# A router and attention kernel with its list building spread over five rounds ahead of the experts instead of four

## What is computed

```python
xn = layernorm(x)
# attention over the 4 heads of the same token, D = 256 per head
q, k, v = (xn @ W + b for W, b in ((Wq, bq), (Wk, bk), (Wv, bv)))
scores = (q*cos . k*cos + q*sin . k*sin) / 16      # per token, head x head
s = softmax(scores) @ v ; s = s.swapaxes(1, 2).reshape(...) @ Wo + bo
# mixture of 8 experts, 2 per token
g = sinkhorn((xn @ router_w.T + router_b) / temp)  # 3 iterations over 8 rows of a sequence
vals, idx = top_k(g, 2) ; w = vals / (sum(vals) + 1e-8)
y = sum_k w[k] * ((relu(xn @ wg[idx]) * (xn @ wp[idx])) @ wo[idx])
out = x + s * silu(xn + y)
```

## Time and profile before

| what | value |
|---|---|
| median of 3 runs | 1592.52 us (1590.27 to 1592.82) |
| profiled execution, its own time | 1590.1 us |
| its span | 1588.3 us |
| TensorE matmul busy | 1530.9 us, 96% |
| VectorE, ScalarE, GpSimd busy | 972.8, 728.8, 793.0 us |
| list matmuls | 128 |

### The profile page before, as it was taken

The page is one execution under the profiler, slowest core; times in us unless marked ns, Lnnn a source line. Parts: engine busy times, 40 slices in busy tenths (PEclk is TensorE's granted clock), DMA queues, the critical chain, the costliest instruction groups (busy, mean ns, idle before and its releaser), DMA issues.

```text
span 1588.3 us, 32794 instructions
## 1 busy us (share of the span) xinstructions
PE 1530.9 (96%) x11408; PEld 1166.3 (73%) x11408; DVE 972.8 (61%) x1880; ACT 728.8 (46%) x1205; POOL 793.0 (50%) x945
## 2 busy tenths in 40 slices
PE   5999699989999999999999999999999999999997
PEld 2546566668888888888888888776666776666773
DVE  7567989953333333333333333577889788888777
ACT  4766334413333333333333333546456565555552
POOL 4637589813433444433444333253574564853456
PEclk9999899989999999999999999999999999999999
DMA  9989852265233231323211231255555666455464
GB/s 327 396 314 324 301 187 78 76 217 189 68 124 108 82 126 64 97 95 111 77 54 57 71 146 51 90 167 166 172 187 189 205 200 207 156 168 172 155 206 147
DMA packets 175351, 251.23 MB, mean 158 GB/s; under 512 B 15336, under 2 KB 122656, under 8 KB 175072
## 3 DMA queue, kind: packets, MB, share of 16 engines
q1 hardware_dynamic: 160576, 211.48, 39.1%
q0 software_dynamic: 12960, 35.41, 6.8%
q10 hardware_dynamic: 1664, 2.26, 0.4%
HBM read 149.58 MB, written 99.50 MB: 157 GB/s over the span
## 4 chain that ended last, share of the span: by engine, by line
PE 89%; DVE 6%; DMA 2%; ACT 1%; issue 1%; SPq 1%; ACTq 0%; DVEq 0%
PE ps L1145 23%; PE ps L1080 21%; PE ps L1091 13%; PE ps L1164 12%; PE ps L1027 6%; PE ps L1154 4%; PE ps L1048 2%; PE ps L1127 2%; PE ps L996 2%; PE ps L924 1%; DMA WR<-w_d 1%; PE ps L980 1%; PE ps L914 1%; DVE UN L1230 1%; SPq L502 1%
## 5 line engine op out<-in xcount | busy, mean ns | idle before, releaser
L1145 PE MATMUL ps<-WR,FR 128*128 x1620 | 407.9, 401 | 1.9 <-DMA WR<-w_d 1.8
L1145 PEld LDWEIGHTS ps<-WR,FR 128*128 128x128 f32 x1620 | 296.2, 189 | 60.2 <-issue 3.0
L649 POOL DMA_INDIRECT y_d<-AUX x135 | 133.3, 987 | 351.6 <-ACT AUX L868 351.6
L1656 DVE TENSOR_TENSOR AUX<-AUX,ps 128x512 f32<-128x512 f32 x135 | 92.9, 688 | 342.0 <-ACT AUX L856 342.0
L817 ACT ACTIVATE WM<-ps,bcs,trig 128x512 f32<-128x512 f32 x256 | 252.2, 1016 | 85.9 <-PE ps L1080 78.9
L1596 DVE TENSOR_SCALAR WM<-ps,vec,trig 128x512 f32<-128x512 f32 x256 | 243.6, 993 | 61.2 <-ACT WM L817 60.5
L1091 PE MATMUL ps<-WM,XTJ 128*128 128x512 f32 x512 | 237.1, 600 | 0.0
L856 ACT ACTIVATE AUX<-ps 128x512 f32<-128x512 f32 x135 | 80.9, 599 | 318.5 <-PE ps L1145 318.5
L1080 PE MATMUL ps<-XH,WH 128*128 128x512 f32 x512 | 204.8, 400 | 6.1 <-issue 3.8
L1164 PE MATMUL ps<-WR,ABR 128*128 x1080 | 209.4, 292 | 0.0
L1080 PE MATMUL ps<-XH,WL 128*128 128x512 f32 x512 | 199.7, 390 | 0.0
(11 more groups left out here) (238 smaller groups left out, 2199.1 us busy)
## 6 DMA issues: line engine op xcount, KB each, us to landing
US<-u_d SPq DMA_DIRECT2D x63, 512.0 KB, 5.4
u_d<-UN SPq DMA_DIRECT2D x120, 256.0 KB, 2.0
WR<-w_d SPq DMA_DIRECT2D x96, 256.0 KB, 6.0
AUX<-y_d SPq DMA_DIRECT2D x32, 512.0 KB, 5.6
WM<-in_L_attn_x_dram SPq DMA_DIRECT2D x16, 512.0 KB, 9.5
xn_d<-WM SPq DMA_DIRECT2D x32, 256.0 KB, 7.3
w_d<-USR SPq DMA_DIRECT2D x16, 512.0 KB, 4.9
AUX<-xn_d SPq DMA_DIRECT2D x16, 512.0 KB, 6.1
```

What stands on the lines that cost most here:

```text
L649: e.indirect_dma_start(y_d, bass.IndirectOffsetOnAxis(toks[:, m - 5:m - 4], 0), YS[:, (m - 5) % 2, :], None).then_inc(s_y[(m - 5) % 2], 16)
L1145: mm = e.matmul(b[:, :], x, WR[:, bass.ds(off[m] + (2048 * z + 1024 * a + 512 * k), 512)], start=(k == 0 and x is xh and z == 0), stop=(k ...
L1656: e.tensor_tensor(HS[:, m % 2, :], GR[:, :], mP[m % 2][:, :], ALU.mult).then_inc(s_h, 1)
```

## The change

QE goes from 4 to 5, and a new QF = 4 keeps the old meaning for the outputs that are made good later: only rounds 0 to 3 are hosted, and round 4 stands ahead of the experts but is finished like the later ones, from round 5 on. In round 4 the U chunks (with the mixes of round 3) come first and the QK chunks last. In rounds 0 to 4 ScalarE writes both halves of chunks 2, 6, 10 and 14, and VectorE leaves them out. The second choice is cut in seven steps, six behind chunks 0 to 5 of round 1 and the gate weights behind chunk 16; the rank matmuls move from behind chunk 1 to behind chunk 8 of round 1, the rank steps to chunks 11 and 13, the slot steps to chunks 0 and 3 of round 2. The list matmuls start at chunk 6 of round 2 and run to chunk 13 of round 4, at most half a matmul for each group of scores. The translation stands behind chunk 15 of round 4, the selectors behind chunks 1, 5, 9 and 13 of round 3, and the permutation behind chunk 20 of round 3, in a bank of its own. Expert 0 is loaded as soon as chunk 23 of round 4, now its eighth, is done.

```diff
-QE = 4
+QE = 5
+QF = QE - 1
+        def order(q):
+            return [*range(16, 24), *range(16)] if q == QE - 1 else list(range(24))
+        def at(q, c):
+            return 24 * q + order(q).index(c) + 1
+        def lone(q, c):
+            return q < QE and c in (2, 6, 10, 14)
...
-            if (q, c) >= (1, 20):
-                pace += 1.5 if c < 16 else 2.4 if c < 24 else 4.0
+            if k >= 34:
+                pace += 1.57 if c < 16 else 2.6 if c < 24 else 0.5
...
-            e.wait_ge(s_ch, 24 * QE)
+            e.wait_ge(s_ch, at(QE - 1, 23))
             load_expert(0)
...
+                            if lone(q, c):
+                                e.activation(rotated(2 * x + 1, i), b, ACT.Identity, bias=bcs[:, x, 1, i:i + 1],
+                                             scale=trig[:, 1, i:i + 1])
...
-            side[24 + 1] = sink_end
+            side[24 + 8] = sink_end
...
+            side[72 + 20] = weigh
...
-            side[21] = top2
-            side[24 + 3] = ranks
-            side[24 + 6] = lambda: slotted(0, oh1)
-            side[24 + 9] = lambda: slotted(1, oh2)
+            for k in range(6):
+                side[24 + k] = lambda k=k: top2(k)
+            side[24 + 11] = lambda: ranks(0)
+            side[24 + 13] = lambda: ranks(1)
+            side[24 + 16] = lambda: top2(6)
+            side[48] = lambda: slotted(0, oh1)
+            side[48 + 3] = lambda: slotted(1, oh2)
             side[48 + 23] = experts
+            for h in range(H):
+                side[72 + 4 * h + 1] = lambda h=h: selector(h)
+            side[72 + 23] = permuted
+            side[24 * (QE - 1) + 15] = listed
...
-                if QE < q < NQ:
+                if q < NQ:
                     total(q - 1)
```

256 lines of the change are left out of this document (137 added, 119 removed).

## The result

The changed kernel takes 1598.24 us (median of five runs, 1597.54 to 1599.49), the kernel before beside it 1592.25 (1589.86 to 1592.82). The ratio is 1.0039, with a 95% interval of 1.0024 to 1.0055: slower by about 6 us, where 8 us faster was forecast. The profiled execution took 1598.14 by its own time, with a span of 1596.4.

The account below looks back on a forecast made before the run. TensorE's own work was taken to bound the kernel, with only front stops to win. Terms -11.4 + 2.3 + 1.9 - 1.5 + 5.3 - 3.3 - 1.3 = -8.0 took 1590.1 to 1582.1 (median up to 1584.5); range 1577 to 1592.

Parts of the forecast that it names:

- Round 0: The second choice leaves round 0, the stop of 10.8 before the mask step shrinks to 0.7: -11.4 us.
- Round 1: VectorE's work moved out of round 0 stands here, with a new stop at the rank matmuls: +2.3, 59.1 us.
- the stop at the rank matmuls: In round 1, behind chunk 8, TensorE waits for VectorE's one-hot sum: a new stop of 4.0 us.
- 19.7: Time in us from round 1's first mix to its end: 22.5 before, less 25 list matmuls of about 0.1.
- given back in full: Rival: round 0's gain is lost as VectorE's queue waits more in round 1 (+7): within 0.2%, near 1591; chance 0.14.
- Round 2: New stop of 2.9 before list matmul 0, 38 list matmuls 3.7, soft stage 0.5, slow clock 1.2: +1.9, 55.4 us.
- Soft stage 0.5: Round 2's allowance of 0.5 us, since the bias step of its last mix still waits for an earlier store.
- Round 3: Translation and selectors leave the first mask step, the gate permutation comes in: -1.5, 55.7 against 57.2 us.
- Round 4: 42 list matmuls +4.1, stop of 2.0 before the scores, translation hidden beside score groups: +5.3, 52.4 us.
- the way into the experts: From last scores to first expert matmul: remainder of tile 0 (2.3) and hand-overs, 3.1 instead of 6.4; -4.6 with clock.
- Behind the experts: Rounds after the experts: change of 0, the twelve bare rounds becoming eleven being counted in round 4's 5.3.
- the slower rival: Clock falls behind five stops of 2 to 4 us, over 11 us above the sum: from 1596 on; chance 0.09.

Follow-up runs that it names:

- experiment 4: Changed kernel with the second choice back in one piece before round 0's first mask step, rank matmuls at chunk 1 of round 1: 1601.04 us, ratio 1.0048.
- 1: Changed kernel with only the 4 MB store of M's second half moved from round 1 to round 3: 1595.37 us, ratio 1.0015 to the kernel before.
- 9: Experiment 8 plus BR loads issued among the weight halves and GpSimd's round 1 XTJ sum behind the last half: 1587.11 us, ratio 0.9969.
- 11: Experiment 9 plus the early output rows finished in odd rounds: 1585.35 us, ratio 0.9948 to the kernel before.
- 12: Changed kernel with queue repairs alone (4 MB store, XB load, BR loads, XTJ sum moved): 1595.28 us, ratio 1.0020 to the kernel before.
- experiment 16: The best kernel: experiment 11 with the changed kernel's own lists (from chunk 6 of round 2, 1.57 a chunk): 1582.87 us, ratio 0.9941.
- 2: Changed kernel with no chunk whole on ScalarE, VectorE having all sixteen half rotations of each of the five rounds: 1604.95 us, ratio 1.0066.
- 3: Changed kernel with the last front round in the usual order, QK first and U last: 1608.68 us, ratio 1.0100 to the kernel before.
- experiment 5: Changed kernel with the experts' first tiles worked out behind chunk 12 of round 2, not its last chunk: 1596.10 us, ratio 1.0020.
- 6: Changed kernel with list matmuls from four chunks later (behind chunk 10 of round 2), a little denser: 1596.29 us, ratio 1.0030.
- experiment 10: Changed kernel with the early output rows finished in rounds 7, 9, 11, 13 instead of 6, 8, 10, 12: 1601.51 us, ratio 1.0055.
- experiment 14: Changed kernel with denser lists (1.66 a chunk), translated behind rotation 11 of round 4, ahead of the scores: 1610.45 us, ratio 1.0108.
- 8: Changed kernel with five repairs: 4 MB store, XB load, rank matmuls (chunk 10), experts' first tiles and lists (chunk 10) moved: 1592.46 us, ratio 0.9998.
- 15: Kernel before with the queue repairs (4 MB store, XB load, BR loads, GpSimd's round 1 XTJ sum moved): 1592.75 us, ratio 1.0007.
- experiment 13: Kernel before with its early output rows finished in rounds 6, 8, 10, 12 instead of 5, 7, 9, 11: 1594.62 us, ratio 1.0023.

## Why the prediction was wrong, step by step

**Round 0 was right.** The mask step stood at 156.33 (forecast 156.7, moved from 166.71) with a stop of 0.61, where 0.7 was forecast. The round took 49.07 for the 48.9 forecast.

**Round 1 is the step that failed first.** The text priced VectorE's queue from the first rotation to the first mix, operation by operation, and let everything behind the mix follow at "19.7". The VectorE part was right and a little too high: the stop at the rank matmuls was 2.35, not 4.0, and the first mix came 37.6 behind the round's start, not 39.4. The term that failed is the 19.7 behind the first mix: it measured 26.4. What the text left out is that SyncE's queue does not start earlier because round 0 ends earlier. The U loads are issued at about 185.5 either way, and behind them stand BR, XB and the 4 MB store. Before, the first mix came at 207.62, when the queue was done; in the changed kernel the mix comes at 198.24 and meets it. The evidence: the second choice put back leaves the end of round 1 at 224.35 (experiment 4); with the store moved (1, 9, 11, 12, 16) the part behind the first mix takes 19.7 to 20.5, and with it where it was (the changed kernel, 2, 3, 5, 6, 10, 14) 22.8 to 27.9, and 21.9 in experiment 4; the BR loads and one sum moved as well bring the first mix itself from 38.1 to 34.1 (8 and 9); and the same repairs are worth nothing in the kernel before (15). In experiment 8 the part behind the mix took 22.9 with the store moved, at half the clock for its first 5.5 us. The rival "given back in full" has 7 us more than the forecast in round 1, and 4.9 came, but for another reason: it blamed VectorE.

Two terms of the text were also added up wrong, by too little to matter: 22.5 less 25 list matmuls of 0.1 is 20.0 and not 19.7, and round 3's terms sum to -1.3 and not -1.5.

**Round 2 failed for another reason.** The stop before list matmul 0 was forecast at 2.9 and was 3.1. "Soft stage 0.5" was mis-sized: I took it from the round before the change, where the experts' step was hidden under 16 list matmuls between the scores. The change took these away, and put GpSimd's XTJ sum beside the step; the stop there measured 2.51, and is gone in experiment 5. The slow clock, priced at 1.2, came to 3.6. The three make up 4.6 of the 4.7.

VectorE's short operations tell what the sum beside them does. Beside GpSimd's sum a tensor_scalar took 1.02 and a cast 1.13, beside its marks 0.32 and 0.10, and the reduction 1.14 both times. The Trainium skill, "SBUF — State Buffer", section "Who interferes with whom", says that copy, cast and tensor_scalar can hold the pair of ports that VectorE shares with GpSimd, and that a tensor_reduce on this chip never does. Beside the sum the trace agrees. Beside the marks nothing was slowed; why this form of GpSimd's work leaves them alone no run shows.

VectorE's soft stage at the end of round 0 took 9.7 (156.33 to 166.07), where I took 10.7: two of its four subtractions took 0.17 or 0.18, two 1.12.

**Round 3, +1.2.** TensorE had no stop here at all (busy for 56.86 of 56.86), and yet its clock was 0.97, 1.7 us lost to it; the text priced none. Experiment 5, which touches nothing in this round, has 1.00 and 55.7, the forecast itself; experiment 1 has 1.00 and 56.6.

**Round 4, +1.7, and the way into the experts, +1.2.** The stop before its scores was 1.76 for the 2.0 forecast. The scores took 9.0 for 7.6. The text says of the translation that "if it were another 1.2 longer it would show", and experiment 14 was to size it, but experiments 1, 4, 5 and 6 (see 14) show that it costs nothing, as forecast: what took the time are the two short stops without a releaser and the matmuls around them. The remainder of tile 0 came 2.4 behind the scores, as forecast (2.3). The hand-overs behind it, priced at 0.8, took 1.9: a second pair of transposes (398.72), a copy and a second remainder (399.58) follow the first one (398.16) before the first expert matmul can start (400.04). In all thirteen changed kernels with U first this matmul comes 4.1 to 4.3 behind the last score, so this is the term that was mis-sized.

**Behind the experts, +3.7.** This was priced at 0. The early output rows went from odd to even rounds, which the text did not see. The expert tiles themselves took 2.0 less than before (657.0 from the first expert matmul to the first row of the next round, for 659.0); the loss is in the rounds behind them. From the first scores behind the experts to the last, the changed kernels with the early rows in even rounds take 473.1 to 481.3 (eleven profiles, the middle one 476.4), the others 472.1 to 474.6 over as many rounds (seven, 472.6); moved in the kernel before, the time rises by 0.23% (experiment 13). The mechanism stays open. The stops without a shown releaser would fit TensorE's program being loaded beside heavy transfers, which is a guess: from 1338 to 1341 the DMA share was 1.05, just ahead of the stop of 2.09. But a transfer of 16 KB on an instruction queue stands ahead of that place in experiment 10 too, with no such stop, moving the rows made the stops vanish without a gain in the median of experiment 10, and in the kernel before it made the loss without the stops.

**The clock** rides on these steps and is inside the rows of the table. In rounds 1 to 3 it was below full speed for 3.2, 3.6 and 1.7 us' worth (0.05, 0.06 and 0.03 of their length), 8.5 where 3.2 was priced. The measured time lies where the slower rival stood (from 1596 on), but not by its mechanism: that asks for over 11 us of slow clock above the sum, and 5.3 came. The kernel before has 10 by the same measure (0.11 of round 0 and 0.06 of round 3), of which half fell into the stops themselves, where TensorE had nothing to slow down (us, then busy (count) PE, PEld, DVE, ACT, POOL, PEclk, DMA, GB/s):

```profile
158.70:167.10 8.40, 0.00 (x0) 0.00 (x0) 8.19 (x10) 0.00 (x0) 6.98 (x8) 0.50 0.93 323
167.20:172.20 5.00, 5.00 (x94) 5.00 (x96) 4.69 (x13) 0.43 (x2) 4.73 (x5) 0.50 1.03 354
```

A stop doesn't set it alone either. Round 2 with the same two stops (3.1, then 2.2 to 2.5) had a granted clock from 1.00 to 0.92 and took 57.1 to 61.1 in five profiles; here are experiments 1 and 4:

```profile
223.03:280.09 57.06, 51.33 (x467) 34.37 (x463) 49.97 (x113) 25.77 (x35) 39.91 (x43) 1.00 0.32 105
```

```profile
224.35:285.47 61.12, 55.42 (x465) 37.43 (x462) 50.91 (x112) 25.79 (x34) 41.06 (x45) 0.92 0.27 95
```

So a price for slow clock behind a stop of this size is a chance and not a sum. In the best kernel, without the stops of the queue, rounds 1 to 3 have 1.00, 0.97 and 1.00.

The single repairs do not add up on their own: 0.24, 0.19, 0.09 and 0.19% for experiments 1, 5, 6 and 12 (which has 1 in it), and 0.98% for experiment 16. Their intervals are some 0.15% to each side, so the medians of single ones carry little. What is solid is that experiment 8, with five repairs, is even with the kernel before (0.9998) and that 9, 11 and 16 are each faster than it (0.9969, 0.9948, 0.9941); those three overlap among themselves.

## What to carry to other kernels

When a change makes a stage end 11 us earlier, write down for the next stage not only what the engines have to do, but the time at which each queue reaches that stage's first transfer: work that runs on its own clock (here weight halves through GpSimd and SyncE) doesn't come forward, and everything behind it in the queue becomes the bound. A step is hidden by what stands beside it, so when a change moves the cover away (here the list matmuls between scores), price the step again. The gain of such a change can be had, but here not by one repair: the same change with two loads, a store and a sum moved in their queues is still 0.20% slower than before, and with the rank matmuls, the experts' step and the early output rows moved too it is 0.59% faster.

## What the runs showed of the hardware

A store of 4 MB that nothing waits for in these rounds took 12.6 us to land, and writes of 256 KB issued behind it in the same queue from 192.7 on landed only at 205.7; with the store moved, no copy waited for them. Whether the order in the queue or the load on the DMA engines held them no run separates. A cast of eight columns took 1.13 us beside a GpSimd addition and 0.10 beside GpSimd's compare-and-multiply marks. TensorE stopped for 1.6 to 2.6 us within a score group with nothing to wait for in the profile; this showed at one or both of the same two places in all eleven changed kernels with the early output rows in even rounds, and in none of the other seven profiles. The granted clock of the same round with the same stops lay between 0.92 and 1.00 from one profile to the next, and once fell to 0.50 (324.5 to 327.5 in the changed kernel) in a round in which TensorE had no stop. And the start of round 0, ahead of everything that these kernels differ in, varied by 7 us between executions.
